# Linear attention of a Perceiver layer on 64x64 quarters of the array: both batches' k^T v in one PSUM bank

## The reference, cut to what matters

```python
q = x @ Wq; k = x @ Wk; v = x @ Wv              # 8 heads of 64
q = jax.nn.softmax(q, axis=-2) * SCALE          # over the 64 numbers of a head
k = jax.nn.softmax(k, axis=-1)                  # as laid out: normalised, then used transposed
context = jnp.einsum('bhdn,bhen->bhde', k, v)   # one 64x64 matrix for each batch and head
out = jnp.einsum('bhde,bhdn->bhen', context, q)
return out.transpose(...).reshape(b, n, HID) @ Wo + bo
```

## Time and profile before

| | us |
|---|---|
| median of 3 runs | 981.15 (978.63 to 981.46) |
| profiled execution | 980.75 |
| its span | 979.0 |
| TensorE busy | 936.0 |
| VectorE busy | 738.2 |
| GpSimd busy | 561.9 |
| ScalarE busy | 503.1 |

### The profile page before, as it was taken

The page is one execution under the profiler, slowest core; times in us unless marked ns, Lnnn a source line. Parts: engine busy times, 40 slices in busy tenths (PEclk is TensorE's granted clock), DMA queues, the critical chain, the costliest instruction groups (busy, mean ns, idle before and its releaser), DMA issues.

```text
span 979.0 us, 18047 instructions
## 1 busy us (share of the span) xinstructions
PE 936.0 (96%) x5988; PEld 805.1 (82%) x5988; DVE 738.2 (75%) x1151; ACT 503.1 (51%) x856; POOL 561.9 (57%) x593
## 2 busy tenths in 40 slices
PE   6999999999999999999999999999998799999998
PEld 3568888888888888888889888888886587888887
DVE  4659778787877977878787797775875667888776
ACT  2557656566565665656646566564442333344332
POOL 5729779678948957967894895610010442444540
PEclk9999999999999999999999999999999799999999
DMA  5872122212211212221221221101005022222200
GB/s 161 271 253 55 51 60 63 53 45 62 63 38 58 66 36 60 62 52 46 60 67 30 58 70 37 51 1 65 1 1 172 5 84 86 87 86 86 86 1 22
DMA packets 75083, 66.40 MB, mean 68 GB/s; under 512 B 7920, under 2 KB 71680, under 8 KB 75008
## 3 DMA queue, kind: packets, MB, share of 16 engines
q1 hardware_dynamic: 75008, 65.37, 22.3%
HBM read 57.48 MB, written 7.86 MB: 67 GB/s over the span
## 4 chain that ended last, share of the span: by engine, by line
PE 85%; DVE 10%; ACT 2%; issue 2%; POOL 1%; DMA 0%; SPq 0%; DVEq 0%; ACTq 0%; POOLq 0%
PE sps L1206 27%; PE scp L1224 9%; PE scp L1226 9%; PE scp L1225 9%; PE scp L1416 5%; PE sps L1402 5%; PE wps L1402 4%; PE scp L1417 3%; DVE u_sb L917 2%; PE wps L1251 2%; DVE st L882 1%; PE sps L1160 1%; PE sps L1319 1%; PE scp L1174 1%; PE sps L1339 1%
## 5 line engine op out<-in xcount | busy, mean ns | idle before, releaser
L1224 PE MATMUL scp<-cn,pt_hi 128*128 128x258 f32 (+1 forms) x832 | 239.2, 288 | 3.6 <-DVE pt_lo L907 2.8
L1225 PE MATMUL scp<-cn,pt_hi 128*128 128x256 f32 (+1 forms) x832 | 234.9, 282 | 0.0
L1226 PE MATMUL scp<-cn,pt_lo 128*128 128x258 f32 (+1 forms) x832 | 234.8, 282 | 0.0
L907 DVE TENSOR_TENSOR pt_lo<-st,pt_hi 128x512 fp32r<-128x512 f32 (+1 forms) x208 | 196.6, 945 | 6.8 <-ACT pt_hi L677 6.8
L668 ACT ACTIVATE st<-sps 128x512 f32<-128x512 f32 (+1 forms) x208 | 123.6, 594 | 148.4 <-PE sps L1206 147.7
L882 DVE TENSOR_TENSOR st<-st,mbc 128x512 f32<-128x512 f32 (+1 forms) x208 | 158.9, 764 | 38.6 <-ACT mbc L691 38.0
L1206 PE MATMUL sps<-qk_hi,ct_hi 128*128 128x512 f32 (+1 forms) x416 | 168.3, 405 | 12.6 <-DVE cmax L893 5.6
L674 ACT ACTIVATE st<-st 128x512 f32<-128x512 f32 (+1 forms) x208 | 130.2, 626 | 88.7 <-DVE st L882 88.2
L1224 PEld LDWEIGHTS scp<-cn,pt_hi 128*128 128x128 f32 (+1 forms) x832 | 156.9, 189 | 13.7 <-DVE pt_lo L907 5.7
L1206 PE MATMUL sps<-qk_hi,ct_lo 128*128 128x512 f32 (+1 forms) x416 | 164.2, 395 | 0.0
L1206 PE MATMUL sps<-qk_lo,ct_hi 128*128 128x512 f32 (+1 forms) x416 | 163.4, 393 | 0.0
(11 more groups left out here) (212 smaller groups left out, 1460.7 us busy)
## 6 DMA issues: line engine op xcount, KB each, us to landing
w_raw<-W SPq DMA_DIRECT2D x16, 1024.0 KB, 7.6
raw<-ctx_t SPq DMA_DIRECT2D x96, 128.0 KB, 2.2
raw<-ctx_n SPq DMA_DIRECT2D x96, 128.0 KB, 2.0
raw<-qk_scratch SPq DMA_DIRECT2D x56, 128.0 KB, 2.0
qk_scratch<-stage_b SPq DMA_DIRECT2D x4, 896.0 KB, 4.7
qk_scratch<-stage_a SPq DMA_DIRECT2D x4, 896.0 KB, 4.5
wq_sb<-w_q SPq DMA_DIRECT2D x1, 1024.0 KB, 5.0
wkt_sb<-w_kt SPq DMA_DIRECT2D x1, 1024.0 KB, 7.9
```

What stands on the lines that cost most here:

```text
L907: dve.tensor_tensor(pt_lo[0:rows(j), r, :], st[0:rows(j), par, j, :], pt_hi[0:rows(j), r, :].bitcast(F32), ALU.subtract).then_inc(lo_ok, 1)
L1224: pe.matmul(scp[:, t, 0:D + 2], hi, cn[0:rows(j), j, 0:D + 2], start=j == 0, stop=False)
L1225: pe.matmul(scp[:, t, 0:D], hi, cn[0:rows(j), j, D + 2:CNW], start=False, stop=False)
L1226: ins = pe.matmul(scp[:, t, 0:D + 2], lo, cn[0:rows(j), j, 0:D + 2], start=False, stop=j == SJ - 1)
```

## The change

k^T v is computed head by head. A matmul takes 64 rows of tokens and 64 columns of k, and its 64x64 result goes to the 64 partitions at which OT wants it: lower heads of a pair to partitions 0 to 63, upper ones to 64 to 127. The result of one batch then fills half a bank, C1 goes to the other half, and one copy without a mask takes both to `cbd`, which is half as large. C1 waits for C0's end on TensorE instead of for a copy. OT takes 64 rows and 64 columns at a time too. The mask, its fills and waits are gone.

```diff
-        bmask = sb("bmask", [P, P])
-        cbd = csb("cbd", [P, 2, 2, HP, P])
+        cbd = csb("cbd", [P, 2, 2, HP, LD])
...
-            link(pool.memset(bmask[:], 0.0))
-            link(pool.memset(bmask[0:Q, 0:Q], 1.0))
-            pool.memset(bmask[Q:P, Q:P], 1.0).then_inc(mask_ok, 1)
-            pool.wait_ge(mask_ok, 1)
...
-                elif o in (8, 9):
-                    b = o - 8
-                    after_pe(("C0", "C1")[b])
-
-                    done(dve.scalar_tensor_tensor(out=cbd[:, r, b, :, :], in0=bank.rearrange("p (t e) -> p t e", e=P),
-                                                  scalar=float(LD) ** -0.5,
-                                                  in1=bmask[:].unsqueeze(1).broadcast_to((P, HP, P)),
-                                                  op0=ALU.mult, op1=ALU.mult))
+                elif o == 9:
+                    after_pe("C1")
+                    done(dve.tensor_scalar(cbd[:, r, :, :, :], bank.rearrange("p (b t e) -> p b t e", b=2, e=LD),
+                                           float(LD) ** -0.5, None, ALU.mult))
...
                     if b == 0:
                         after_act("lqT")
                     else:
-                        after_dve("cbd0")
-                    rows = slice(b * Q, (b + 1) * Q)
+
+                        pe.wait_ge(chain_pe[m], PE_NO["C0"])
+                    rows = head_rows[b]
                     for t in range(HP):
-                        ins = pe.matmul(bank[:, t * P:(t + 1) * P], kn[rows, r, t * P:(t + 1) * P],
-                                        v_sb[rows, r, t * P:(t + 1) * P], start=True, stop=True)
+                        for hr in head_rows:
+                            h = slice(t * P + hr.start, t * P + hr.stop)
+                            n0 = (b * HP + t) * LD
+                            ins = pe.matmul(bank[hr, n0:n0 + LD], kn[rows, r, h], v_sb[rows, r, h],
+                                            start=True, stop=True)
                     done(ins)
                 elif o == 10:
-                    after_dve("cbd1")
+                    after_dve("cbd")
                     for t in range(HP):
                         for b in range(2):
-                            ins = pe.matmul(bank[:, t * P + b * Q:t * P + (b + 1) * Q], cbd[:, r, b, t, :],
-                                            lqT[:, r, t, b * Q:(b + 1) * Q], start=True, stop=True)
+                            for hr in head_rows:
+                                ins = pe.matmul(bank[hr, t * P + b * Q:t * P + (b + 1) * Q], cbd[hr, r, b, t, :],
+                                                lqT[hr, r, t, b * Q:(b + 1) * Q], start=True, stop=True)
                     done(ins)
```

More of the change, by code:

```diff
@@ L327, in build @@
         chain_pool = [sem(f"chain_pool{m}") for m in range(MT)]
-        mask_ok = sem("mask_ok")
         eidx_ok = sem("eidx_ok")
@@ L1069, in _ @@
             dve.wait_ge(tanh_ok, 1)
-            dve.wait_ge(mask_ok, 1)
             dve.wait_ge(eidx_ok, 1)
@@ L1504 @@
 ACT_NO = number("lnT exp_k exp_q v kn lqT lo_T lnT_hi lnT2 exp_diff")
-DVE_NO = number("o+b x1 stats1 aggr1 eps1 ln1 kmax ksub qmax qsub ksum krec kmul qsum qrec qmul cbd0 cbd1 "
+DVE_NO = number("o+b x1 stats1 aggr1 eps1 ln1 kmax ksub qmax qsub ksum krec kmul qsum qrec qmul cbd "
                 "y+b x2 stats2 aggr2 eps2 ln2 lnT_lo logit top diff index topf 1+e w0 w1 gw0 sel gw")
```

## The result

The changed kernel took 976.08 us (median of 7 runs, 972.43 to 976.98), the kernel before 980.77 beside it (7 runs, 978.63 to 981.46): a ratio of 0.995, interval 0.9934 to 0.9966. So near a hit needs the next rows before it is believed.

The account below looks back on a forecast made before the run. TensorE, busy 96% of the span, was taken as the bound, with the late engine judged tile by tile. Gains 1.2 + 1.05 + 1.45 + 1.0 = 4.7 us gave 976.3 us, range 972.5 to 981.0.

Parts of the forecast that it names:

- Pace on quarters, 34 ns: C0, C1 and OT as 64x64 matmuls: 34 ns a record, so 0.55 us less per C and 0.64 per OT.
- Rival 1: In OT, row halves writing one PSUM bank take turns: 68 ns a record, 0.3 us gained together, 980.7 us; chance 0.14.
- Rival 2: In every C and OT, loads on quarters are not hidden: 138 ns a record, about 999.7 us; chance 0.05.
- m0, 1.2: First tile: 1.2 us less, C0's 0.55 and OT's 0.64, with C1's gain lost behind pt_lo.
- m1, 1.05: Second tile: 1.05 us less, C1's 0.55 and OT's 0.64 less 0.15, with C0's gain lost.
- The 0.15 that I took off for the copy: In m1, 0.15 us deducted because the copy ends just when the earlier OT wants to start and pt_lo binds.
- m2, 0.8 for the wait: Third tile: C1 leaves the chain, VectorE normalises m3 then makes one copy; OT starts 0.8 us sooner, 756.4 against 757.19.
- m3, the 0.35 before OT: Fourth tile: C0 and C1 give 1.1 us, but the copy ends at 791.65, so OT starts only 0.35 us sooner.
- The copy, 0.7 to 0.8: On VectorE, one unmasked copy per tile costs 0.7 to 0.8 us, replacing two masked ones: 0.55 to 0.7 us less.
- The clock, "about 17 us": Expected in the trace after: TensorE's low clock in about 17 us.
- the forecast's own range: Range given to the forecast itself, 974.8 to 977.8 us; chance 0.50.
- the shorter dip: Clock rival: the first low-clock stretch is shorter or gone, time down to 972.9 us; chance 0.10.

Follow-up runs that it names:

- e3_grouped: The changed kernel with the same matmuls reordered, those of one quarter in a row, in k^T v and OT: 978.79 us, ratio 0.9971 to the kernel before.
- the pair at full clock: Changed kernel and kernel before, each with 37 unused 128x128 matmuls added ahead of five TensorE waits in m2 and m3: 971.61 and 977.87 us.
- e0_after: The changed kernel once more, no edit: 973.97 us, ratio 0.993 to the kernel before.
- e6_act_copy: The changed kernel with the one copy of k^T v on ScalarE instead of VectorE: 973.21 us, ratio 0.9923 to the kernel before.

## Why the prediction was right, point by point

- **Pace on quarters, 34 ns: right.** OT 34, C 38 (0.61 us for the 0.54 forecast, which over eight products is 0.5 us; 0.07 us each). The nearest row in size and in its pattern of turns, L1251, was the right one to go by. e3_grouped shows that the pattern was half of that reason: without turns, the same shapes take 57.
- **Rival 1, halves that take turns at one bank: wrong.** OT writes one bank from both row halves, in turn, at 34 ns a record. The Trainium skill, "TensorEngine Tiling (Array Packing)", section "Gotcha 1: PSUM Pressure", says that different row tiles cannot access one bank at the same time; on two quarters that write different partitions the pace here shows no cost of that. Two row halves that write the same partitions at once are the case not tried.
- **Rival 2, loads that are not hidden: wrong.** It needed 75 ns a record; the slowest order measured has 57.
- **m0, 1.2: 0.98.** C0 gives 0.48 instead of 0.55, OT 0.65; of these 1.13 us 0.15 do not arrive. The two traces place 0.14 of them around OT: from the last product with the context to OT's start it is 0.22 us with the change and 0.12 before, and from the transposes behind OT to the next product 0.41 against 0.37. The forecast had no term for going over to another shape, and what in it takes the time was not tested. The covered part was named rightly: C1's gain is lost behind pt_lo, for which the load behind it waits 1.15 us (up to 1.2 forecast, 0.69 before):
```profile
706.97 0.19 PEld L1212 LDWEIGHTS scp<-cn,pt_hi 128*128 128x128 f32 x1 [1.15 <-DVE pt_lo L900]
```
- **m1, 1.05: 1.07.** C0's gain is lost, C1's and OT's are there. The 0.15 that I took off for the copy is not needed: it ends at 720.33, and OT starts at 721.00 without a wait. C1 gives 0.47 instead of 0.55 and OT starts 0.07 us later behind the product ahead of it, so the sum is right with other parts.
- **m2, 0.8 for the wait: 0.86, and 0.91 with fillers.** I had VectorE normalise at 755.3 and then copy. The chain of waits after (start, us, what) shows the same two in this order, earlier by what m0 and m1 gave:
```profile
752.86 0.56 POOL rstd L596
...
753.44 0.41 DVE ln_out L974
...
753.86 0.61 DVE cbd L1017
...
754.51 1.15 PE sps L1362 x32
```
The copy is behind the normalisation and GpSimd's reciprocal root, as forecast, so one copy and one product are off the chain.
- **m3, the 0.35 before OT: the step that failed.** C0 and C1 give nothing. I took the subtraction on GpSimd, and with it h_hi and the copy, as fixed in time while TensorE came sooner, and left 0.35 of TensorE's lead. The 0.35 was read in a trace in which TensorE had just run at half clock: there the copy was done before TensorE came. At full clock there is no such slack, and the kernel before itself waits for the copy. In the pair at full clock OT waits 1.35 us for the copy with the change and 0.40 without it: that is 0.95 more, of the 2 x 0.48 us that the shorter C0 and C1 free, so all of it is turned into that wait. The changed kernel itself, whose clock is low until about 776.6, waits 0.53 us (0.57 in e0_after) where I expected 0.7, and shows the chain:
```profile
779.67 2.37 POOL L602 TENSOR_TENSOR w_lo<-w_raw,w_hi 128x1024 fp32r<-128x1024 f32 x1 [5.34 <-ACT w_hi L756]
...
780.53 1.74 DVE L1069 CAST h_hi<-h_f 128x384 fp32r<-128x384 f32 x1 [0.90 <-ACT h_f L763]
783.64 0.69 DVE L1017 TENSOR_SCALAR cbd<-scp 128x512 f32<-128x512 f32 x1
784.38 1.15 PE L1362 MATMUL scp<-ke,cbd 64*64 64x64 f32 x32 [0.53 <-DVE cbd L1017]
```
h_hi starts beside the subtraction and ends just behind it, at 782.3, after 1.74 us, where others of its line take 0.36; then come the pairs and the copy. e6_act_copy takes the copy out of this queue, and the wait is gone.
- **The copy, 0.7 to 0.8: 0.68 us,** just under the range, and no shorter than a copy with the mask (0.68 too), so what VectorE saves is one whole copy per tile. L840, at 806 ns, reads two columns of scalars, this one a constant; no run shows that this is the difference.
- **The clock, "about 17 us": wrong in its size.** The traces of the changed program have 6.8 and 13.6 us, and a run at 0.991 some 17.6 (an estimate, twice 0.009 of its 975 us). At an equal clock the terms sum to 4.3 to 4.4, where I had 4.7. So the hit to 0.2 us is luck: the median of the first seven runs came out at 976.1 because four of them had the long low stretches, and over all twelve it is 974.8, inside the forecast's own range but only just. The chance for the shorter dip, 0.10, was too small: by their mean clock 8 of the 12 runs had it to some degree. For OT of m2 I took it that a low stretch lasts a time and not an amount of work; no run separates the two, and the first stretch is 6.8 us before, 3.4 in e0_after and absent in the other trace.

What stays open is why the changed kernel has the long stretches less often (4 of 12 runs at 0.991 and none below, against 38 of 42 at 0.991 or below). The waits of TensorE in m2 and m3 matter, since filling them takes the low stretches of this part away in both kernels; that the change's own effect goes by the wait it removes in m2 was only argued.

## What to carry to other kernels

Small products on quarters of the array are worth writing so that neighbours in the program use different quarters; measured here, the same matmuls cost 34 ns a record in turns and 57 in a row, which for OT decides between a gain and none. When a product gets faster, look at the queue of the engine whose copy it feeds: in m3 nearly all of the faster k^T v went into a longer wait, and moving that copy to an engine with room gave it back and more (1.35 us there, 1.6 in all). Where low-clock stretches of a few us fall in or near the changed part, compare runs by their clock or fill the waits in both kernels, since one trace against one trace reads 8.3 us here (980.75 and 972.43) for a gain of 4.4.

## What the runs showed of the hardware

- 64x64 products with 64 moving columns in float32, two quarters in turn: 34 ns (OT) to 38 ns (C) a record with loads of 135 ns; the same quarter again and again 56 to 57 ns (e3_grouped). Halves of rows and of columns taking turns together (OT) are no faster than halves of columns alone (L1251, 34 ns): the 17 ns that I left open as a lower bound do not occur.
- 37 matmuls without use, some 9 us of TensorE's time placed in its waits (12 of their records take 1.60 us), made both kernels faster: by about 3 us at the median in each (974.81 to 971.61, and 981.05 to 977.87), as the granted clock rose from a mean of 0.991 to 0.996 up to 0.998 to 1.00.
- Of one program, runs at a mean clock of 0.991 and 0.996 differ by 4 us (976.73 and 972.69): by an estimate from the two means about 10 us more at half speed, and four tenths of them lost.
